# Eight value tiles projected before the key combine, which goes by column blocks, and six weight units kept in SBUF between two passes

## The chip, the cores and the metric

The kernel runs on the 8 cores of one Trainium2 chip. Each core computes 2048 of the 16384 rows of the output. Within a batch row of 4096 positions two cores share the work: both form the whole key-value sum for all 4096 rows, and each does the query side and the feed-forward part for its own half. No data pass between cores. The metric is the device time of the slowest core, in microseconds (us).

Names used below: TensorE is the matmul engine (PE in the profile), VectorE is DVE, ScalarE is ACT, GpSimd is POOL, SyncE is SP, which issues most of the DMA transfers. SBUF is the memory on the core, PSUM the matmul's result memory of 8 banks.

## The reference, cut to what matters

```python
x = x + attn(layernorm(x))          # x: (4, 4096, 1024) float32, 16 heads of 64
x = x + ffn(layernorm(x))

def attn(h):
    q = softmax((h @ Wq.T + bq) @ Wfq.T + bfq)    # over all 1024 columns
    k = softmax((h @ Wk.T + bk) @ Wfk.T + bfk)
    v = h @ Wv.T + bv
    scores = q_h @ k_h.T                           # per head, no softmax here
    return (scores / scores.sum(-1)) @ v_h

def ffn(h):                                        # weights 1024 x 4096 and back
    gate = silu(bitlinear(h, w_gate)); up = bitlinear(h, w_up)
    return bitlinear(gate * up, w_down)

def bitlinear(x, w):      # x rounded to 8 bit by row; w to {-1, 0, 1} / scale,
    ...                   # scale = 1 / mean(|w|) over the whole matrix
```

Two things follow. The two matrices of the key can be multiplied once, Wfk Wk, and so can those of the query. And since the attention has no softmax over scores, it is q (k^T v), so a 64 x 64 sum per head over all positions takes the place of the scores. The feed-forward weights need two passes: one over |w| for the mean, one that rounds with that mean.

## The kernel before, in words

The work is cut into tiles of 128 rows. A core has TKV = 32 tiles for the keys and values (16 of the other core's half, then its own 16), and TQ = 16 for the queries and the feed-forward part. All engines' programs are written out by hand as lists in order, each instruction with the events that it waits for. An engine does its list strictly in order, so an instruction that waits holds up all behind it.

First stage, weights. SyncE loads the weights in chunks of at most 128 x 1024 float32 into 8 staging buffers (`stage`), and VectorE and ScalarE cast them to bf16 in turns (`cast_chunk`, L275 and L277). Chunks 0 to 23 are Wk and Wfk, then come Wv and, from 32 on, Wq and Wfq, which overwrite the first two and so wait for the bias product BK. The key combine (L435) is 128 matmuls in two passes of 64: for each half h of the output columns all eight PSUM banks collect one row block each, while j runs over the chunks as they land. `cke` (L807, L810) copies the results out. Then come the bias item BK and the first keys.

Second stage, slots. Slot i of 32 has, on TensorE, V(i) (value projection), in slots 16 to 26 Q, in slots 4 to 12 one item of the query combine (CQ, L415 with wfT), K(i+1), the KV product of tile i (L464) and the transposes of tile i+2 (L453). Each of V, K, Q and CQ is an "item" of 16 matmuls of 128 x 512 that takes one of two PSUM areas of two banks. VectorE and ScalarE do for each tile: mean and variance (`dv_stats`), r = exp(-0.5 ln(var + eps)) (`ac_r`, L728 and L732), the normalized tile (`dv_xh`, L738), the copy of its transpose (`dv_xte`, L745), logits with bias (`dv_tk`, L750), their maximum (L754), the exponential with its sum (`ac_ek`, L1068), the reciprocal of the sum (`dv_rz`, L785) and V scaled by it (`ac_ve`, L1077 and L1084), for which the KV product waits.

The units. The feed-forward weights come in 48 units of 1 MB (16 of each matrix, w = 0 gate, 1 up, 2 down). In pass 1 ScalarE sums |w| of a unit (L335), in pass 2 GpSimd scales and rounds it (L326) and ScalarE writes it as fp8 (L348). Both passes load each unit from HBM into one of NWST = 4 buffers (`wst`). A table gives each slot its units, 74 up to slot 31: 3 a slot in slots 3 to 8, 2 in 9 to 15, 3 in 16 to 25, 2 in 26 to 31. The other 22, of the down matrix, follow in the feed-forward tiles 0 to 3.

Third stage. After slot 31 come the last queries, the first context product (L522) and 16 feed-forward tiles: gate and up (L563), silu (L1136), the product (L1013), rounding, a transpose through HBM (`s_hq`), and down (L543), three tiles late.

Of the kernel before, what the change touches and what calls it, by code (L numbers as in the profile page):

```python
# [93 lines left out]
def build_nc():  # L94
# [147 lines left out]

    chunks = []
    for j in range(CH):
        chunks += [("wk", j, 0, D, wnat), ("wfkT", j, 0, 512, wfT)]
    chunks += [("wfkT", j, 512, 512, wfT) for j in range(CH)]
    chunks += [("wvT", j, 0, D, wv) for j in range(CH)]
    for j in range(CH):
        chunks += [("wq", j, 0, D, wnat), ("wfqT", j, 0, D, wfT)]
    NK, NV = 24, 32  # L250
    chunk_id = {(c[0], c[1], c[2]): n for n, c in enumerate(chunks)}

    def cast_of(name, j, o=0):
# [1009 lines left out]
```

How the kernel before makes its waits and increments, by code:

```python
    def run(self, eng, e, sems):  # L75
        seen = {}
        for fn, after, sem, by in self.lists[eng]:
            need = {}
            for tok in after:
                assert tok.val is not None, tok.name
                if tok.val > seen.get(tok.sem, 0):
                    need[tok.sem] = max(need.get(tok.sem, 0), tok.val)
            seen.update(need)
            need = list(need.items())
            for s, v in need[:-1]:
                e.wait_ge(sems[s], v)
            inst = fn(e)
            if need:
                inst.wait_op(sems[need[-1][0]], need[-1][1], "sem-ge")
            if sem:
                inst.then_inc(sems[sem], by)
```

## Time and profile before

| | us |
|---|---|
| median of 3 runs | 1144.21 |
| lowest, highest | 1143.06, 1147.94 |
| the profiled execution | 1148.11 |
| its span, slowest core (4) | 1146.6 |
| its fastest core (1) | 1123.3 |
| TensorE busy, core 4 | 1080.8 (94%) |
| VectorE, ScalarE, GpSimd busy | 632.1, 491.1, 204.4 |

A span runs from a core's first to its last instruction. The profile is that of core 4. Matmuls are pipelined and their ends are modelled, so TensorE's busy time is not work at peak rate; the start of one group of matmuls to the start of the next is the better measure. The granted clock is given as a share of 2.4 GHz: 0.50 is the lower level, 1.2 GHz. Some matmul records are missing from a trace, which is why an item can stand there with x15.

### The profile page before, as it was taken

To read this page: it belongs to the slowest core of one execution; us is meant where nothing else is said; L and a number is where in the kernel's file an instruction comes from. 1 tells how busy PE (TensorE), PEld (TensorE's weight loads), DVE (VectorE), ACT (ScalarE), POOL (GpSimd) and SP (SyncE) were. 2 spreads that over 40 slices of the span, in tenths; PEclk is the share of its full clock that TensorE was granted. 3 is DMA by queue.
4 is the path that set the end of the run, shared out by engine and by line. 5 is a ranking of instruction groups with operands and counts; after the bars stand their busy time and mean duration, and the time that the engine had idled before them with its cause. 6 is when DMAs were issued, how large, how long until landed. Compare 5 with 4: busy or idle time off the path is not lost.

```text
span 1146.6 us, 13483 instructions; the slowest of 8 cores (1123.3 to 1146.6 us)
## 1 busy us (share of the span) xinstructions
PE 1080.8 (94%) x5379; PEld 503.7 (44%) x5414; DVE 632.1 (55%) x1140; ACT 491.1 (43%) x604; POOL 204.4 (18%) x132
## 2 busy tenths in 40 slices
PE   5859999999999999897879999999999999999998
PEld 2324454554444544342334444444444444444443
DVE  3356555667766667774826636645645645744311
ACT  2326776677787757564533123223223222222110
POOL 0000000023333330453322012012012012011010
PEclk9979899999998999998989999999999999999999
DMA  8969998689999977779971441441342351231240
GB/s 271 290 198 339 338 334 294 244 276 325 316 325 324 326 222 220 183 215 191 170 132 37 111 96 42 101 108 40 92 105 52 83 120 37 74 92 37 56 110 38
DMA packets 201263, 199.66 MB, mean 174 GB/s; under 512 B 170096, under 2 KB 170096, under 8 KB 193008
## 3 DMA queue, kind: packets, MB, share of 16 engines
q1 hardware_dynamic: 179392, 174.68, 54.2%
q10 hardware_dynamic: 21808, 24.12, 7.5%
q8 instruction: 42, 0.69, 0.3%
q14 instruction: 21, 0.17, 0.1%
HBM read 148.45 MB, written 29.36 MB: 155 GB/s over the span
## 4 chain that ended last, share of the span: by engine, by line
PE 79%; DMA 10%; DVE 4%; ACT 3%; POOL 2%; issue 1%; SPq 1%; ACTq 0%; DVEq 0%
PE ps L563 32%; PE ps L415 25%; PE ps L543 19%; DMA wst<-wdT 4%; DMA stage<-wfkT 2%; DMA wst<-wgT 2%; DMA bvb<-bv 2%; PE ps L464 1%; PE ps L453 1%; SPq L233 1%; ACT wd L348 1%; POOL hmid L1186 1%; POOL wst L326 1%; DVE hmid L1013 1%; DMA xr<-x_oth 1%
## 5 line engine op out<-in xcount | busy, mean ns | idle before, releaser
L563 PE MATMUL ps<-wg,aqT 128*128 128x512 fp8e4 x1024 | 244.9, 382 | 8.6 <-ACT silu L1136 6.0
L563 PE MATMUL ps<-wu,aqT 128*128 128x512 fp8e4 x1024 | 243.2, 381 | 4.1 <-DVE hmid L1013 4.1
L1136 ACT ACTIVATE silu<-ps,l 128x512 f32<-128x512 f32 x128 | 87.7, 686 | 319.5 <-PE ps L563 302.4
L1013 DVE SCALAR_TENSOR_TENSOR hmid<-ps,l,silu 128x512 f32<-128x512 f32 x128 | 95.7, 748 | 146.4 <-PE ps L563 102.2
L326 POOL TENSOR_SCALAR wst<-wst,msum 128x2048 f32<-128x2048 f32 x48 | 95.9, 2001 | 398.6 <-DMA wst<-wgT 292.5
L563 PEld LDWEIGHTS ps<-wu,aqT 128*128 128x128 bf16 x1024 | 100.2, 98 | 127.3 <-DVE hmid L1013 6.3
L563 PEld LDWEIGHTS ps<-wg,aqT 128*128 128x128 bf16 x1024 | 98.8, 99 | 122.4 <-ACT silu L1136 7.1
L415 PE MATMUL ps<-wck,xT 128*128 128x512 bf16 x509 | 127.8, 408 | 13.8 <-DVE xT L745 11.3
L1186 POOL TENSOR_SCALAR hmid<-hmid,hsc 128x1024 f32<-128x1024 f32 x64 | 70.4, 1118 | 306.2 <-DVE hsc L1034 306.2
L415 PE MATMUL ps<-wv,xT 128*128 128x512 bf16 x484 | 116.2, 392 | 5.7 <-ACT ek L1068 3.9
L1005 DVE SCALAR_TENSOR_TENSOR xr<-ps,hsc,xr 128x512 f32<-128x512 f32 x32 | 24.0, 751 | 168.3 <-PE ps L543 168.3
L1146 ACT ACTIVATE hqs<-hmid 128x1024 bf16<-128x1024 f32 x64 | 66.9, 1056 | 71.1 <-POOL hmid L1186 69.8
L335 ACT ACTIVATE wst<-wst 128x2048 f32<-128x2048 f32 x48 | 91.2, 1900 | 6.6 <-DMA wst<-wgT 5.2
L543 PE MATMUL ps<-wd,hqTa 128*128 128x512 fp8e4 x384 | 86.7, 387 | 6.5 <-ACT wd L348 6.5
L415 PEld LDWEIGHTS ps<-wck,xT 128*128 128x128 bf16 x512 | 52.6, 104 | 83.5 <-issue 33.8
L1021 DVE TENSOR_REDUCE hmx<-hmid 128x1 f32<-128x1024 f32 x64 | 78.1, 1220 | 2.2
L415 PEld LDWEIGHTS ps<-wv,xT 128*128 128x128 bf16 x512 | 50.1, 100 | 61.5 <-issue 13.2
L750 DVE TENSOR_TENSOR lg<-ps,bkc 128x1024 f32<-128x1024 f32 x32 | 39.2, 1224 | 60.9 <-PE ps L415 60.9
L1179 POOL TENSOR_TENSOR xr<-xr,bvb 128x1024 f32<-128x1024 f32 x16 | 38.1, 2387 | 184.7 <-DMA xr<-x_own 184.7
L543 PE MATMUL ps<-wd,hqTb 128*128 128x512 fp8e4 x320 | 69.9, 379 | 0.0
L543 PEld LDWEIGHTS ps<-wd,hqTa 128*128 128x128 bf16 x384 | 38.0, 99 | 54.2 <-ACT wd L348 7.9
L415 PE MATMUL ps<-wcq,xT 128*128 128x512 bf16 x254 | 60.6, 394 | 1.2 <-DVE hmid L750 1.1
(95 smaller groups left out, 1064.6 us busy)
## 6 DMA issues: line engine op xcount, KB each, us to landing
wst<-wgT SPq DMA_DIRECT2D x32, 1024.0 KB, 10.6
wst<-wuT SPq DMA_DIRECT2D x32, 1024.0 KB, 9.0
wst<-wdT ACTq DMA_DIRECT2D x19, 1024.0 KB, 7.0
xr<-x_own SPq DMA_DIRECT2D x32, 512.0 KB, 6.9
s_hq<-hqs SPq DMA_DIRECT2D x32, 512.0 KB, 4.1
wst<-wdT SPq DMA_DIRECT2D x13, 1024.0 KB, 8.9
xr<-x_oth SPq DMA_DIRECT2D x16, 512.0 KB, 12.1
y<-xr SPq DMA_DIRECT2D x16, 512.0 KB, 3.4
```

Source lines behind the costliest of these rows:

```text
L326: gp(lambda e: e.tensor_scalar(b, b, msum[:, 4 + w:5 + w], ROUND32, op0=ALU.mult, op1=ALU.add), [at("wld", n), at("scale", w)], ("usc", n))
L335: ac(lambda e: e.activation(b, b, ACTF.Abs, bias=0.0, scale=1.0, accum_out=absc[:, k:k + 1]), [at("wld", n)], ("unit", n))
L415: pe(lambda e, h=h, c=c, l_=l_, r_=r_: e.matmul(AB[b][:, 512 * h:512 * h + 512], l_, r_, start=(c == 0), stop=(c == CH - 1)), (list(after) ...
L543: pe(lambda e, c=c, b=b, o=o: e.matmul(KB[1 + h], b[:, o:o + 128], wd8[:, c * D + 512 * h:c * D + 512 * h + 512], start=(c == 0), stop=(c ...
L563: pe(lambda e, c=c: e.matmul(out, a[:, c * 128:c * 128 + 128], w8[:, c * DI + 512 * oc:c * DI + 512 * oc + 512], start=(c == 0), stop=(c = ...
L750: dv(lambda e: e.tensor_tensor(o, b, bias[...], op=ALU.add), after, done)
L1013: dv(lambda e: e.scalar_tensor_tensor(hmid[:, 512 * oc:512 * oc + 512], U[oc % 2], l2[:, s + 6:s + 7], sl, op0=ALU.mult, op1=ALU.mult), [a ...
L1021: dv(lambda e: e.tensor_reduce(hmx[:, s2 + k:s2 + k + 1], hmid[:, D * k:D * k + D], axis=AX, op=ALU.max, apply_absolute_value=True), [at(" ...
L1136: ac(lambda e: e.activation(silu[:, (oc % 2) * 512:(oc % 2) * 512 + 512], G[oc % 2], ACTF.Silu, bias=0.0, scale=l2[:, s + 5:s + 6]), [at(" ...
L1146: ac(lambda e: e.activation(hqs[:, g * D:(g + 1) * D], hmid[:, g * D:(g + 1) * D], ACTF.Copy, bias=-ROUND32, scale=1.0), [at("hr", t, g)] ...
L1179: gp(lambda e: e.tensor_tensor(xf(t), xf(t), bvb[...], op=ALU.add), [at("x2in", t), at("biases")], ("xb", t))
L1186: gp(lambda e: e.tensor_scalar(o, o, hsc[:, k:k + 1], ROUND32, op0=ALU.mult, op1=ALU.add), [at("hs", t)], ("hr", t, g))
```

## The change

Four things are changed.

- Loading order. x and Wv come first, interleaved, then Wfk, then Wk, then the key's bias (on a semaphore of its own), Wq and Wfq. Wk comes in column blocks: a chunk is 512 rows by 256 columns, so its rows are 1 KB long. All eight Wv casts are ScalarE's.
- V of tiles 0 to 7 (NE = 8) is projected before the combine. V0 to V3 are interleaved by landing, one bank pair for each tile. V4 to V7 follow as items, each with the transposes of the next tile ahead of it. The results are copied unscaled to SBUF as float32 (`vra`, `vrb`; L910 of the changed kernel for ScalarE), and `ac_ve` scales them from there in slots 0 to 7. `vrb` lies in the first two unit buffers.
- The key combine is eight items, one for each row block of the result, each of which needs all of Wfk and one column block of Wk.
- Units. The up matrix goes first. Units 13 to 15 of up and of gate (NRET = 3) go in pass 1 to places of their own (`keep`), in the regions where the fp8 weights will lie later, and pass 2 takes them from there without a load; the sum's unneeded output goes to `junk`. The first NB = 8 units share buffers 2 and 3. The 74 units are dealt to slots by weights of 4 for each item: 1, 1, 2, 2, 2, 3, 4, 3, 3, 3, 3, 3, 2 in slots 3 to 15, then 3, 3, 3, 4, 3, 3, 3, 3, 4, 3, 3, 2, 2, 3 in slots 16 to 29, and none in 30 and 31. The query combine is one slot later.

```diff
+NE = 8
...
+NRET = 3
...
+    vra = sb("vra", 4 * D, F32, rWC)
+    vrb = sb("vrb", 4 * D, F32, rWS)
...
+    chunks += [rows("wvT", j, wv) for j in range(CH)]
+    chunks += [rows("wfkT", j, wfT) for j in range(CH)]
+    chunks += [block(b, h) for b in range(4) for h in range(2)]
...
+        return n >= 8 and (n % 2 == 0 if n < NV else n % 4 != 3)
...
+    units = [(1, w, u) for w in (1, 0) for u in range(16)]
+    kept = list(range(16 - NRET, 16))
+    own = [(2, w, u) for w in (1, 0) for u in kept + list(range(16 - NRET))]
...
+    cq_slot = {5 + m: m for m in range(9)}
+    slot_len = [4 + (4 if i >= NE else 0) +
+                (4 if i in cq_slot or TQ <= i < TKV - DEFER else 0)
+                for i in range(TKV - 2)]
+    slot_units = {i: [] for i in range(TKV)}
+    for n in range(NA):
+        want = sum(slot_len[:3]) + (n + 1) * sum(slot_len[3:]) / NA
+        slot_units[next(i for i in range(TKV - 2) if sum(
+            slot_len[:i + 1]) >= want - 1e-6)].append(n)
...
+    NB = len([n for n in range(NA) if unit_slot[n] < NE])
+    wslot_of, k = [], 0
+    for n, (ps_, w, u) in enumerate(units):
+        if w < 2 and u in kept:
+            wslot_of.append(None)
+        elif n < NB:
+            wslot_of.append(2 + n % 2)
+        else:
+            if n == NA:
+                k = 0
+            wslot_of.append(k % (NWST if n < NA else NWF))
+            k += 1
...
+                     at("VE", 2 * s + 5) if s < 2 else None)
...
+            k = units[n][2] - 16 + NRET
+            return keep[units[n][1]][:, k * 2048:(k + 1) * 2048]
...
+        if wslot_of[n] is None:
+            if ps_ == 1:
+                sp(f"dR{w}{u}", dst, unit_src(w, u), ready[w], ("wld", n))
+            return
...
+            o = junk[...] if wslot_of[n] is None else b
...
-    for h in range(2):
-        for j in range(CH):
-            for mi in range(CH):
-                pe(lambda e, j=j, mi=mi, h=h: e.matmul(
-                    ps[:, 512 * mi:512 * mi + 512],
-                    wnat[:, j * D + mi * 128:j * D + mi * 128 + 128],
-                    wfT[:, j * D + 512 * h:j * D + 512 * h + 512],
-                    start=(j == 0), stop=(j == CH - 1)),
-                   [cast_of("wk", j), cast_of("wfkT", j, 512 * h),
-                    at("CKe", mi, 0) if h and j == 0 else None],
...
+    def pe_v4(i, j):
+        for h in range(2):
+            pe(lambda e, h=h: e.matmul(
+                ps[:, 1024 * i + 512 * h:1024 * i + 512 * h + 512],
+                xT_of(i)[:, j * 128:j * 128 + 128],
+                wv[:, j * D + 512 * h:j * D + 512 * h + 512],
+                start=(j == 0), stop=(j == CH - 1)),
+               [at("XTe", i), cast_of("wvT", j)] if h == 0 else (),
+               ("V", i) if h == 1 and j == CH - 1 else None)
+
+    x_in = [9.9, 12.9, 16.3, 21.1]
+    w_in_at = [9.8, 11.4, 14.6, 16.2, 19.4, 21.0, 22.6, 24.2]
+    order4 = [(x_in[i] - 1.4, i, -1) for i in range(4)]
+    order4 += [(max(x_in[i], w_in_at[j]), i, j) for i in range(4)
+               for j in range(CH)]
+    for _, i, j in sorted(order4):
+        if j < 0:
+            pe_xt4(i)
+        else:
+            pe_v4(i, j)
...
+    pe_xt(4)
+    for i in range(4, NE):
+        if i + 1 < NE:
+            pe_xt(i + 1)
+        pe_v(i)
+    for m in range(CH):
+        item(("CK", m), lambda c, m=m: wnat[:, c * D + m * 128:
+                                            c * D + m * 128 + 128],
+             w_rhs(wfT), [cast_of("wfkT", 7), cast_of("wfkT", 6),
+                          cast_of("wk", 2 * (m // 2)),
+                          cast_of("wk", 2 * (m // 2) + 1)],
+             ("CK", m), at("CKe", m))
+    item("BK", brep_lhs(0), w_rhs(wfT), [at("brep", 0)], ("BK",), at("BKe"))
     pe_k(0)
-    pe_xt(1)
     pe_k(1)
     for i in range(TKV):
-        pe_v(i)
+        if i >= NE:
+            pe_v(i)
...
+    sp("dC0", identb[...], id_b.ap())
+    load_x(0)
+    load_x(1)
+    load_chunk(0)
+    load_chunk(1)
+    load_x(2)
+    load_chunk(2)
+    load_chunk(3)
+    load_x(3)
+    sp("dC0", identh[...], id_h.ap(), (), ("ids",))
+    for n in range(4, 8):
         load_chunk(n)
+    for i in range(4, NE):
+        load_x(i)
     sp("dC2", b8[:, 0:CH], bk8.ap())
     sp("dC2", b8[:, CH:2 * CH], bq8.ap(), (), ("b8",))
-    for n in range(8, NK):
+    for n in range(8, NV):
...
+    def v_raw(i):
+        b = (ps[:, 1024 * i:1024 * i + 1024] if i < 4 else
+             AB[item_bank[("V", i)]])
+        evac("v" if i == 2 else "a", vraw(i), b, [at("V", i)], ("VR", i))
+
+    def cke(m):
+        evac("v" if m % 2 == 0 else "a", wck[:, m * D:(m + 1) * D],
+             AB[item_bank[("CK", m)]], [at("CK", m)], ("CKe", m))
+
+    def dv_in(i):
+        dv_stats(i)
+        ac_r(i)
...
+    casts = [[0], [1, 2], [3], [4, 5, 6, 7]]
+    for i in range(4):
+        dv_in(i)
+        for n in casts[i]:
+            cast_chunk(n)
+        dv_xte(i)
+    v_raw(0)
+    dv_in(4)
+    v_raw(1)
+    v_raw(2)
+    dv_xte(4)
+    v_raw(3)
+    for i in range(5, NE):
+        dv_in(i)
+        dv_xte(i)
+        cast_chunk(2 * i - 2)
+        cast_chunk(2 * i - 1)
+        v_raw(i - 1)
     dv_brep(0)
     dv_brep(1)
+    cast_chunk(14)
+    cast_chunk(15)
+    v_raw(NE - 1)
+    for n in range(16, 20):
         cast_chunk(n)
+    cke(0)
+    cke(1)
+    cast_chunk(20)
+    cast_chunk(21)
+    cke(2)
+    cke(3)
+    cast_chunk(22)
+    cast_chunk(23)
+    for m in range(4, CH):
+        cke(m)
...
+        b = vraw(i) if i < NE else AB[item_bank[("V", i)]]
```

How the lists change. TensorE before, from its first matmul (wfT, wnat: the key combine; wck: K; wv: V; vst, ek: KV):

```order
L435 MATMUL ps<-wfT,wnat 128x512 x128
L415 MATMUL ps<-wfT,brep 128x512 x16
L453 MATMUL ps<-identb,xh 128x128 x8
L415 MATMUL ps<-wck,xT 128x512 x16
L453 MATMUL ps<-identb,xh 128x128 x8
L415 MATMUL ps<-wck,xT 128x512 x16
L415 MATMUL ps<-wv,xT 128x512 x16
L464 MATMUL ps<-vst,ek 128x129 x8
```

TensorE now, from the end of V3 to the first K of slot 1 (xT_84 to xT_87 are tiles 4 to 7, xT_80 is tile 0):

```order
L539 MATMUL ps<-identb,xh 128x128 x16
L483 MATMUL ps<-wv,xT_84 128x512 x16
L539 MATMUL ps<-identb,xh 128x128 x8
L483 MATMUL ps<-wv,xT_85 128x512 x16
L539 MATMUL ps<-identb,xh 128x128 x8
L483 MATMUL ps<-wv,xT_86 128x512 x16
L483 MATMUL ps<-wv,xT_87 128x512 x16
L483 MATMUL ps<-wfT,wnat 128x512 x128
L483 MATMUL ps<-wfT,brep 128x512 x16
L483 MATMUL ps<-wck,xT_80 128x512 x16
L483 MATMUL ps<-wck,xT_81 128x512 x16
L550 MATMUL ps<-vst,ek 128x129 x8
```

The combine has moved behind eight value projections, and slots 0 to 7 have no V of their own any more.

ScalarE now, from the copy of V0 (vra, vrb: unscaled V; lnv and rr: Ln and Exp for the next tile's normalizing; wfT: casts of Wfk chunks). The first row of L910 is V0, the x2 are V1 and V3, then V4 and V5:

```order
L910 ACTIVATE vra<-ps 128x1024
L831 ACTIVATE lnv<-mv,cst 128x1
L835 ACTIVATE rr<-lnv 128x1
L910 ACTIVATE vra<-ps 128x1024 x2
L831 ACTIVATE lnv<-mv,cst 128x1
L835 ACTIVATE rr<-lnv 128x1
L309 ACTIVATE wfT<-stage 128x1024
L910 ACTIVATE vrb<-ps 128x1024
L831 ACTIVATE lnv<-mv,cst 128x1
L835 ACTIVATE rr<-lnv 128x1
L309 ACTIVATE wfT<-stage 128x1024
L910 ACTIVATE vrb<-ps 128x1024
```

The Ln and Exp of tile 6 stand behind the copy of V4, those of tile 7 behind the copy of V5. In before, no copy of V stood on this queue ahead of slot 0; its start was casts and copies of the combine's results.

## Rows read from the trace of the kernel before

**Rows 1.** Spans: core, first to last instruction, mean granted TensorE clock.

```profile
...
core 4: 1146.6 us, clock 0.969
...
die 0 (median of its cores): 1125.9 us, clock 0.986
die 1 (median of its cores): 1136.2 us, clock 0.974
```

**Rows 2.** Windows, core 4: busy time by engine, TensorE's clock, DMA share, GB/s.

```profile
50.00:100.00 50.00, 33.27 (x165) 15.47 (x170) 26.48 (x41) 16.47 (x28) 0.00 (x0) 0.81 0.81 253
100.00:150.00 50.00, 47.41 (x250) 22.75 (x252) 28.29 (x40) 37.33 (x51) 0.00 (x0) 0.93 1.00 335
250.00:300.00 50.00, 49.72 (x269) 24.42 (x271) 33.69 (x42) 39.75 (x44) 17.76 (x9) 0.92 0.92 297
```

**Rows 3.** Waits of TensorE, 0 to 130 us: total, times, longest.

```profile
...
PE ps L415 <- DVE xT L745: 11.3, 2, 10.2
...
```

**Rows 4.** TensorE in time, core 4: start, duration, line, operation, [idle before, releaser].

```profile
86.63 3.62 PE L415 MATMUL ps<-wck,xT 128*128 128x512 bf16 x15
90.09 0.63 PE L464 MATMUL ps<-vst,ek 128*128 128x129 bf16 x8
90.56 0.64 PE L453 MATMUL ps<-identb,xh 128*128 128x128 bf16 x8
91.02 4.37 PE L415 MATMUL ps<-wv,xT 128*128 128x512 bf16 x16
...
117.21 5.31 PE L415 MATMUL ps<-wck,xT 128*128 128x512 bf16 x16 [2.38 <-ACT vst L1084]
...
130.35 4.38 PE L415 MATMUL ps<-wck,xT 128*128 128x512 bf16 x16
...
239.37 3.62 PE L415 MATMUL ps<-wv,xT 128*128 128x512 bf16 x15
...
417.27 0.63 PE L522 MATMUL ps<-kvs,eld 128*128 128x130 bf16 x8
```

**Rows 5.** ScalarE, core 4: the last of the first 16 weight chunks.

```profile
26.67 0.63 ACT L277 ACTIVATE wfT<-stage 128x512 bf16<-128x512 f32 x1 [2.25 <-DMA stage<-wfkT]
```

**Rows 6.** VectorE in time, core 4, 27 to 135 us.

```profile
49.78 0.69 DVE L745 COPY xT<-ps 128x1024 bf16<-128x1024 bf16 x1 [2.93 <-PE ps L453]
50.39 0.80 DVE L738 TENSOR_SCALAR xh<-xr,mv,rr 128x1024 bf16<-128x1024 f32 x1
...
65.38 1.28 DVE L719 BATCH_NORM_STATS2 bnst<-xr 128x6 f32<-128x512 f32 x2
...
85.25 1.29 DVE L275 CAST wnat<-stage 128x1024 bf16<-128x1024 f32 x2
...
90.29 1.23 DVE L750 TENSOR_TENSOR lg<-ps,bkc 128x1024 f32<-128x1024 f32 x1 [2.32 <-PE ps L415]
91.55 1.22 DVE L754 TENSOR_REDUCE nm<-lg 128x1 f32<-128x1024 f32 x1
```

**Rows 7.** ScalarE in time, core 4, 27 to 135 us.

```profile
44.59 2.06 ACT L810 ACTIVATE wck<-ps 128x512 bf16<-128x512 f32 x4 [0.97 <-PE ps L435]
...
66.94 0.30 ACT L728 ACTIVATE lnv<-mv,cst 128x1 f32<-128x1 f32 x1 [18.41 <-DVE mv L722]
...
67.37 1.99 ACT L277 ACTIVATE wv<-stage 128x1024 bf16<-128x1024 f32 x2
...
92.80 1.15 ACT L1068 ACTIVATE ek<-lg,nm 128x1024 bf16<-128x1024 f32 x1 [2.39 <-DVE nm L754]
...
106.66 1.90 ACT L335 ACTIVATE wst<-wst 128x2048 f32<-128x2048 f32 x1
...
115.91 1.11 ACT L1077 ACTIVATE vst<-ps,rz 128x1024 bf16<-128x1024 f32 x1 [0.23 <-DVE rz L785]
```

**Rows 8.** Windows of 2.5 us, core 4.

```profile
92.50:95.00 2.50, 2.50 (x12) 1.02 (x10) 1.79 (x5) 1.24 (x2) 0.00 (x0) 0.81 1.01 341
117.50:120.00 2.50, 2.50 (x7) 0.87 (x6) 1.58 (x3) 2.07 (x5) 0.00 (x0) 0.50 1.01 331
```

**Rows 9.** TensorE in time, core 1.

```profile
115.19 3.63 PE L415 MATMUL ps<-wck,xT 128*128 128x512 bf16 x16 [2.54 <-ACT vst L1084]
```

**Rows 10.** DMA issues of the page: count, KB each, median us to landing.

```profile
wst<-wgT SPq DMA_DIRECT2D x32, 1024.0 KB, 10.6
...
s_hq<-hqs SPq DMA_DIRECT2D x32, 512.0 KB, 4.1
```

More of the change, by code:

```diff
@@ L191, in build_nc @@
     wst = sb("wst", NWST * 2048, F32, rWS)
+    keep = [sb("keep0", 4 * 2048, F32, rWG), sb("keep1", 4 * 2048, F32, rWU)]
+    junk = sb("junk", 2048, F8, rJK)
     xr2 = sb("xr2", 2 * D, F32, rWS + 8192 * (NWST - 1))
@@ L301, in build_nc @@
     unit_id = {k: n for n, k in enumerate(units)}
-    wslot_of = [n % NWST if n < NA else (n - NA) % NWF
-                for n in range(len(units))]
+    cq_slot = {5 + m: m for m in range(9)}
[7 more added lines that the diff above has]
+            slot_len[:i + 1]) >= want - 1e-6)].append(n)
+    unit_slot = {n: i for i, l in slot_units.items() for n in l}
+    NB = len([n for n in range(NA) if unit_slot[n] < NE])
[10 more added lines that the diff above has]
+            k += 1
     before = {}
     for n, s in enumerate(wslot_of):
+        if s is None:
+            continue
         earlier = [m for m in range(n) if wslot_of[m] == s]
-        before[n] = at("unit", earlier[-1]) if earlier else None
+        before[n] = (at("unit", earlier[-1]) if earlier else
+                     at("VE", 2 * s + 5) if s < 2 else None)
     last_x = max(m for m in range(len(units)) if wslot_of[m] == NWST - 1)
@@ L327, in unit_gp @@
                 b, b, msum[:, 4 + w:5 + w], ROUND32, op0=ALU.mult,
-                op1=ALU.add), [at("wld", n), at("scale", w)], ("usc", n))
+                op1=ALU.add),
+                [at("unit", unit_id[1, w, u]) if wslot_of[n] is None else
+                 at("wld", n), at("scale", w)], ("usc", n))
+    last_junk = [None]
     def unit_ac(n):
@@ L340, in unit_ac @@
             after = [at("usc", n)]
-            if w == 0 and u == 0:
-                after += [at("CQ", 8)]
-            if w == 1 and u == 0:
-                after += [at("cast", len(chunks) - 1),
-                          at("cast", len(chunks) - 2)]
+            if w < 2 and u == 16 - NRET:
+                after += ready[w]
             if w == 2 and u == 0:
@@ L373, in mean_dv2 @@
             op0=ALU.mult), [at("mean", w)], ("deq", w))
-    slot_units = {}
-    n0 = 0
-    for i in range(TKV):
-        left, slots = (32 - n0, TQ - i) if i < TQ else (NA - n0, TKV - i)
-        k = 0 if i < 3 else -(-left // slots)
-        slot_units[i] = list(range(n0, n0 + k))
-        n0 += k
     ffn_units = {}
@@ L389, in build_nc @@
     assert n1 == len(units)
-    unit_slot = {n: i for i, l in slot_units.items() for n in l}
     mean_at = {unit_slot[unit_id[1, w, 15]] + 1: w for w in range(2)}
@@ L399, in build_nc @@
     late_q = list(range(TQ - DEFER, TQ))
-    cq_slot = {4 + m: m for m in range(9)}
     item_no = [0]
-    bank_free = [at("CKe", 1, 1), at("CKe", 3, 1)]
-    also_free = [at("CKe", 0, 1), at("CKe", 2, 1)]
+    bank_free = [at("VR", 0), at("VR", 1)]
     item_bank = {}
@@ L417, in item @@
                     start=(c == 0), stop=(c == CH - 1)),
-                   (list(after) + [bank_free[b], also_free[b]])
+                   (list(after) + [bank_free[b]])
                    if h == 0 and c == 0 else (),
@@ L567, in pe_half @@
                after if c == 0 else (), done if c == CH - 1 else None)
-    WL = unit_id[2, 1, 15]
+    WL = max(unit_id[2, w, u] for w in range(2) for u in range(16))
     def ctx_bank(t, part):
```

179 lines of the change are left out of this document (84 added, 95 removed).

## Prediction

> **What bounds the kernel now.** I read the spans and clocks of the cores first. The time is that of the slowest core, number 4 with 1146.6 us, on the die whose clock is lower ([rows 1]). The profiled execution took 1148.11 us, 1.5 more than that span and 3.9 more than the median of the runs shown, so the sum below gives a difference, and I take it from 1144.2. Within 0.5%, 5.7 us, is what a measurement of this kernel can't tell from no change.
>
> Next I read the busy time by stage ([rows 2]). TensorE is busy for 99% of 250 to 300 us, and no wait of it stands in 130 to 400, but for 33 of 50 us in the window from 50. The first 130 us are therefore where idle time of TensorE can be won. The list of waits names the largest piece: 10.2 us of one wait for a transposed tile ([rows 3]), which stands behind the bias broadcasts that all share one semaphore. The order in time ([rows 4]) gives what I compare. The projections are items of 16 matmuls (8 for the key combine, one for its bias, 9 for the query's, 32 V, 32 K, and 13 of the 16 Q before the first context product at 417.27): 95 in all. An item takes 90.09 - 86.63 = 3.46 us, a KV product 0.47, a transpose group 0.46. When K6 starts, at 130.35, 72 of the 95 are left. In the changed order 72 are left when slot 5 begins (V0 to V7, eight combines, the bias, K0 to K5 are done). So one question decides most: is that before or after 130.35?
>
> **The change part by part: V0 to V3.** They follow the landings of x and wv. By the row where 6 MB are cast, 26.67, they would end some 2.7 us later, at 29.4 ([rows 5]). At the 335 GB/s of [rows 2] the chunks, now of 512 KB and all with whole rows, land by 22 to 23. Then TensorE itself is the limit: after x3 (4 MB in, its stats, normalizing, transpose and copy, about 21) 28 matmuls are left, 6 us. I take 27.2, and keep 25.2 and 29.4 as ends. All four V results then wait for VectorE and ScalarE.
>
> **V4 to V7.** The instruction order shows a ring here: ScalarE copies V(i-1) out of PSUM before it does the Ln and Exp for tile i+1, so XH(i+1), the transpose and then V(i) on TensorE's queue wait for V(i-1). From [rows 6] and [rows 7]: copy 1.03 (2.06 for 4 halves, two halves each), Ln and Exp 0.43 (67.37 - 66.94), XH 0.80, some 0.4 of semaphores, transposes 0.46, V itself 3.46: 6.6 us a tile, where TensorE's own work is 3.9. V4 comes first after: V0 copied 26.9, Ln and Exp for tile 4 27.4, XH 28.3, the VectorE copy of V2 29.5, transposes 30.1, XT 30.8, stats of tile 5 32.3 (1.56 from 65.38 to 66.94), Ln and Exp 32.9, XH 33.7, transposes, V4 from 34.3. Its gap is over 3 us, and such gaps have a price: after 2.38 us of wait at 117.21 the K item took 5.31 instead of 3.62, with a granted clock of 0.50, the 1.2 GHz level ([rows 4, 8]); on core 1 2.54 us of wait cost nothing ([rows 9]). So V4 ends at 34.3 + 3.4 + 1.7 = 39.4. V5 begins after 1.1 + 0.5 + 0.9 + 0.5 of copy, Ln, XH and transposes at 42.4, V6 at 48.9, V7 at 52.3, ending 55.7. The gaps before V5 and V6 are 2.6 us, between the two cases named, so I charge 1.7 us for one of them. ScalarE copies V7 and casts one more chunk: 56.8, 57.8. The key combine starts at 57.9, or at 59.6 with the charge.
>
> **The key combine.** It is 8 items, 27.6 us, then the bias item 3.5 and K0 3.4: K0 ends at 92.4. Its column blocks are loaded in rows of 1 KB, which no row of before shows. The bounds are 1.6 us for 512 KB at 335 GB/s and 4.1 us from issue to landing for the same size in rows of 256 B ([rows 10]). With either end eight of them take 13 to 33 us from 36 on, so the last pair, issued near 56, is there by 64, and is needed at 79: zero in both cases. The combine covers it; if it landed 15 us later still, it would be one for one.
>
> **Slots 0 to 4.** TensorE has only K and KV there (3.9 us), while each slot's chain is: logits 1.26, maximum 1.25, exponential 1.28, reciprocal 0.1, three casts on VectorE 1.9 ([rows 6, 7]): 5.8 us. V is already there but its scaling (1.11) still follows the exponential. K0 end +9.4 for the first KV (K1, then 5.5 us of gap, as two exponentials go ahead of it on ScalarE), K2 with a low clock +14.5, KV2 +20.3, KV3 +26.1, KV4 +31.9. So 72 are left at 124.3, with the charge at 126.0. That is 4.3 us ahead of 130.35. The 27.7 us of V work that moved into the time of loading come back almost whole as gaps: some 8 before V4, 5 before V5 and V6, 2 before the combine, 5.5 + 5 in the slots, and the lost clock.
>
> **Slots 5 to 31.** The items are the same as before, 28 to the V16 that started at 239.37, and 44 from there on. The first eight units have only two buffers. A buffer's round is landing + 1.90 for the absolute sum ([rows 7]) + 0.4 of issue. With 2.5 MB in flight at 335 GB/s each load lands 5 to 6 us after issue, the round is about 8, and the slot 7.4 to 7.9. I add 1 us. Slots 8 to 15 load 24 units and 4 MB of x in 83 us, 337 GB/s, just what [rows 2] shows as the most, but up to four units are ahead when it starts, and slot 16 loads none: zero. The six units kept save 6 MB, 18 us of transfers, from slot 16 on. On core 4 no wait of TensorE is there to be removed, so they are worth nothing to the slowest core. Slots 30 and 31 have no unit on ScalarE, where before it had two each; that frees the KV evacuation: -1 us. From 417.27 on (wd units, the hidden-tile transposes, 16 tiles) nothing differs. The junk output and the added work on POOL (none) cost nothing.
>
> **The sum.** -4.3 + 1 - 1 = -4.3 us: span 1142.3 of the profiled execution, and 1144.2 - 4.3 = 1140 as median. Its own range: the ends of V3 (-2 to +2.2), the two gaps (-1.7 to +1.7), the buffers (-1 to +2) give 1135 to 1145.
>
> **The rivals.**
> - The clock comes back in the second half (faster). Core 4 has 0.92 in three windows of 50 us from 250 on (the first stands in [rows 2]), while the other die's median is 10 us shorter ([rows 1]). If fewer transfers, or the other placing of ScalarE's units, give it full clock, 150 x 0.08 = 12 us go: 1128. Against: the items there, back to back, stay the same.
> - The buffers of the first eight units (slower). Place: slots 5 to 8, ScalarE. In before such a load took 10.6 us in the median from issue to landing ([rows 10]). With that, a round is 13 us for two units where the slot has 7.8: 5.2 x 3 = 15.6, less the 4 us that K runs ahead of KV, so 12 more: 1151. It decides from a landing of about 5.5 us. For it: the 2.38 us wait at 117.21 arose in just this way, behind a unit on ScalarE's queue. Against: 10.6 us was with four buffers in flight.
> - What is won is used up in the start (no difference). Both gaps before V5 and V6 fall to the low clock, those of 1.5 to 1.9 us in slots 2 to 4 too, and slot 14, with three units for 7.8 us of TensorE, adds 1 us: 1144 to 1145.
> - The denser stretch costs clock (slower than forecast). Core 4 was granted 0.81 at 92.5 to 95 us in dense matmuls ([rows 8]). Slots 5 to 15 should take 28 x 3.46 + 11 x 0.93 = 107.1 us and took 109.0 (130.35 to 239.37, [rows 4]), so 1.9 are lost there now. If the stretch runs at 0.92, as 250 to 300 does, 109 x 0.08 = 8.7 are lost, 6.8 more: 1147. For it: TensorE and the DMA queues are both busier there than before. Against: 150 to 250 us of before is as dense and lost little. The Trainium skill, in "TensorE: Matmul & The Clock Gate", Part 1: The HAM clock gate, has a peak-current limit of 13/16 of the clock for a die once three of its cores run dense matmuls. This trace agrees in the value, but not in the duration. Held over the 109 us, that rule would give 1140 + 20.7 - 1.9 = 1159.
>
> **How the numbers follow.** The forecast has 0.39, the returned clock 0.22, the used-up start 0.14, the buffers 0.15, the denser stretch 0.05, and 0.05 goes to something slower that is not on the list. Faster by over 0.5% means under 1138.5: 0.19 of the forecast's own share and the 0.22, so 0.41. Slower means over 1149.9: the buffers, 0.02 of the denser stretch, and the unlisted: 0.22. The rest, 0.37, is within. The range for 8 in 10 goes from the returned clock to the buffers, 1127 to 1151.
>
> **What would show it.** In the profile after: V4 starting near 34 and the combine near 58 to 60, with ScalarE's Ln between the V copies; gaps of 2.6 us before V5 and V6; a gap of some 5.5 us before the first KV; the first query combine (slot 5) at 124 to 128; V16 near 234 to 236; the first context product near 413; the same distance from there to the end, 729 us. Wrong it is if V5 and V6 follow without gaps (then the start gives 5 us more), if ScalarE waits for wst in slots 5 to 8 for more than 2 us a unit, if the clock of the second half is not 0.92, or if the wk blocks land after 79.

## The result, and the profile after

The changed kernel is slower: 1176.28 us in the median (1172.75 to 1235.38, 4 runs) against 1146.08 for the kernel before in the same runs. The ratio is 1.026, with a 95% interval of 1.0215 to 1.031. The forecast was 1140, the range ended at 1151. (The 1235.38 and a few long runs of the kernel before are disturbed ones, with a lower granted clock on one die or both; they stand in the medians, but in no ratio.)

The spans after (for [rows 1]): every core is longer than the median of either die before, and the clocks of the dies are alike.

```profile
core 4: 1171.0 us, clock 0.977
...
die 0 (median of its cores): 1159.8 us, clock 0.980
die 1 (median of its cores): 1167.8 us, clock 0.980
```

From each trace the four times below were read on all eight cores and their median formed: when slot 5's share of work is reached (72 of the 95 items left), the start of V16, the first context product, and the end. The differences from column to column tell where time is lost.

| kernel | time, median | 72 left | V16 | context | end |
|---|---|---|---|---|---|
| before | 1146.08 | 127.8 | 235.5 | 411.9 | 1130.4 |
| changed | 1176.28 | 149.4 | 262.6 | 443.0 | 1160.7 |
| difference | +30.2 | +21.6 | +27.1 | +31.1 | +30.3 |

So 21.6 us are lost before slot 5, 5.5 in slots 5 to 15, 4.0 up to the context product, and nothing behind it. The waits of TensorE over the whole span (total, times, longest) already name the places (for [rows 3]):

```profile
PE ps L550 <- ACT vst L1208: 22.0, 6, 8.6
PE ps L505 <- DMA identh<-id_h: 19.7, 1, 19.7
PE ps L483 <- ACT vst L1208: 9.5, 5, 3.7
PE ps L539 <- DVE xh L841: 8.4, 3, 3.6
```

L505 are the transposes of tiles 0 to 3: 19.7 us until an identity matrix lands. L550 are the KV products. The order in time on core 4 (for [rows 4]; the last 34 matmuls of V0 to V3, V4, transposes, V5, transposes, V6 and V7, combine, KV of tile 4, first query combine, V16, context product):

```profile
37.07 7.50 PE L513 MATMUL ps<-wv,xT 128*128 128x512 bf16 x34
...
51.87 5.72 PE L483 MATMUL ps<-wv,xT 128*128 128x512 bf16 x16
59.97 0.62 PE L539 MATMUL ps<-identb,xh 128*128 128x128 bf16 x8 [2.38 <-DVE xh L841]
60.43 3.62 PE L483 MATMUL ps<-wv,xT 128*128 128x512 bf16 x16
66.42 1.03 PE L539 MATMUL ps<-identb,xh 128*128 128x128 bf16 x8 [2.38 <-DVE xh L841]
67.25 8.32 PE L483 MATMUL ps<-wv,xT 128*128 128x512 bf16 x32
77.72 27.79 PE L483 MATMUL ps<-wfT,wnat 128*128 128x512 bf16 x128 [2.15 <-ACT wnat L309]
...
150.72 1.05 PE L550 MATMUL ps<-vst,ek 128*128 128x129 bf16 x8 [8.63 <-ACT vst L1208]
151.56 5.37 PE L483 MATMUL ps<-wfT,wnat 128*128 128x512 bf16 x16
...
265.42 3.62 PE L483 MATMUL ps<-wv,xT 128*128 128x512 bf16 x16
...
446.78 0.63 PE L620 MATMUL ps<-kvs,eld 128*128 128x130 bf16 x8
```

Part of this came out as worked out, and part did not. V4 to the combine is 77.72 - 51.87 = 25.9 us (25.3 in the prediction), with gaps of 2.38 us before the transposes for V5 and V6. Behind one of the two equal gaps the clock stayed up (16 matmuls from 60.43 in 3.62), behind the other it was low at first (32 from 67.25 in 8.32, where 7.07 is full speed). But V4 itself starts at 51.87, not 34.3. And the KV of tile 4 has an idle time of 8.63 us ahead of it, where 5.8 - 3.9 = 1.9 were expected. SyncE's queue (start, time, issues) shows both causes:

```profile
6.26 0.61 SPq L249 DMA_DIRECT2D identh<-id_h  x1
...
10.26 25.26 SPq L249 DMA_DIRECT2D xr<-x_oth  x4
...
36.51 5.99 SPq L249 DMA_DIRECT2D stage<-wfkT  x8
...
93.72 0.33 SPq L249 DMA_DIRECT2D stage<-wfqT  x1
119.48 0.33 SPq L249 DMA_DIRECT2D stage<-wq  x1
...
126.36 0.53 SPq L249 DMA_DIRECT2D wst<-wuT  x1
```

The loads of x4 to x7 take from 10.26 to 35.5, as each waits for a normalized tile, and the Wfk chunks stand behind them. The ninth Wq/Wfq chunk waits from 94 to 119 for the buffer of the first, whose cast waits for the bias item. That item is done at 109; the cast then stands on VectorE behind the logits and maxima of tiles 0 and 1 and comes at 118.77. So the first feed-forward unit (wst) is issued only at 126.36, behind eight chunks and two biases of 512 KB each that were all issued after 119. ScalarE then waits for it, with the exponential of the next tile behind:

```profile
146.02 1.91 ACT L413 ACTIVATE wst<-wst 128x2048 f32<-128x2048 f32 x1 [7.09 <-DMA wst<-wuT]
```

The identity matrices (count, KB, us to landing): the same 32 KB took 1.9 us when issued first and 13.4 when issued behind x and Wv, and the first transposes wait for both, as they share a semaphore.

```profile
identb<-id_b SPq DMA_DIRECT2D x1, 32.0 KB, 1.9
identh<-id_h SPq DMA_DIRECT2D x1, 32.0 KB, 13.4
```

The windows (for [rows 2]) show the transfer queues at 170 GB/s in 100 to 150, where before they ran at 335, and ScalarE at 41 to 42 of 50 us in 300 to 400. TensorE's clock in 250 to 300 is 1.00. That it was 0.92 on one die of the kernel before belongs to that execution: in four later kernels (units only; units and bias; units, bias, spread; bias only) the mean clock of 250 to 400 us was 0.98 to 1.00 on every core.

```profile
100.00:150.00 50.00, 33.55 (x170) 15.55 (x168) 22.94 (x30) 18.37 (x26) 0.00 (x0) 0.91 0.57 170
250.00:300.00 50.00, 50.00 (x292) 25.02 (x291) 34.11 (x51) 40.48 (x51) 7.89 (x4) 1.00 0.90 290
300.00:350.00 50.00, 46.03 (x260) 22.23 (x258) 30.81 (x42) 41.03 (x46) 19.50 (x10) 1.00 1.02 322
350.00:400.00 50.00, 48.14 (x269) 23.21 (x268) 33.27 (x42) 42.07 (x45) 20.46 (x11) 1.00 0.94 292
```

### The profile page after: what moved, and what is told of

Its sections match the earlier page's. It is cut to its first block, busy times and chain, and to the rows that moved or that the text cites. A ratio compares the mean times of both kernels' runs of the same rounds, so it can differ in the third digit from the quotient of the medians.

```text
span 1171.0 us, 13492 instructions; the slowest of 8 cores (1156.7 to 1171.0 us)
## 1 busy us (share of the span) xinstructions
PE 1076.2 (92%) x5414; PEld 503.2 (43%) x5414; DVE 624.4 (53%) x1133; ACT 499.8 (43%) x603; POOL 204.4 (17%) x132
## 4 chain that ended last, share of the span: by engine, by line
PE 61%; DMA 16%; ACT 8%; issue 7%; DVE 4%; POOL 3%; SPq 1%; ACTq 0%; DVEq 0%; POOLq 0%
PE ps L661 30%; PE ps L641 18%; PE ps L483 9%; DMA wst<-wuT 6%; DMA wst<-wdT 4%; DMA wst<-wgT 3%; POOL wst L399 2%; DMA keep<-wuT 2%; ACT wu L427 1%; DMA identh<-id_h 1%; PE ps L513 1%; ACT wst L413 1%; ACT wd L427 1%; ACT ek L1191 1%; ACT wg L427 1%
## 5 line engine op out<-in xcount | busy, mean ns | idle before, releaser
L483 PE MATMUL ps<-wck,xT 128*128 128x512 bf16 x512 | 118.4, 386 | 9.5 <-ACT vst L1208 9.5
L399 POOL TENSOR_SCALAR wst<-wst,msum 128x2048 f32<-128x2048 f32 x42 | 84.1, 2004 | 191.5 <-DMA wst<-wuT 93.2
L483 PE MATMUL ps<-wv,xT 128*128 128x512 bf16 x448 | 106.9, 394 | 0.0
L413 ACT ACTIVATE wst<-wst 128x2048 f32<-128x2048 f32 x42 | 79.9, 1902 | 20.4 <-DMA wst<-wuT 16.4
L483 PEld LDWEIGHTS ps<-wck,xT 128*128 128x128 bf16 x512 | 49.6, 99 | 73.3 <-ACT vst L1208 15.1
L483 PEld LDWEIGHTS ps<-wv,xT 128*128 128x128 bf16 x448 | 44.3, 101 | 50.8 <-issue 7.6
L483 PE MATMUL ps<-wfT,wnat 128*128 128x512 bf16 x256 | 58.5, 387 | 2.1 <-ACT wnat L309 2.1
L483 PE MATMUL ps<-wcq,xT 128*128 128x512 bf16 x256 | 57.7, 379 | 1.1 <-DVE hmid L853 1.1
```

What stands on the lines that cost most here:

```text
L399: gp(lambda e: e.tensor_scalar(b, b, msum[:, 4 + w:5 + w], ROUND32, op0=ALU.mult, op1=ALU.add), [at("unit", unit_id[1, w, u]) if wslot_of[ ...
L413: ac(lambda e: e.activation(o, b, ACTF.Abs, bias=0.0, scale=1.0, accum_out=absc[:, k:k + 1], saturate=False), [at("wld", n), last_junk[0] ...
L483: pe(lambda e, h=h, c=c, l_=l_, r_=r_: e.matmul(AB[b][:, 512 * h:512 * h + 512], l_, r_, start=(c == 0), stop=(c == CH - 1)), (list(after) ...
```

## The experiments

Each kernel was run beside the kernel before, in four groups in which that kernel's median was 1144.7 to 1146.6. The ratio is to those runs, and it can differ from the quotient of the medians by some tenths of a per cent. The four times on the right are medians of the eight cores of one profiled execution.

| kernel | time | ratio, 95% | 72 left | V16 | context | end |
|---|---|---|---|---|---|---|
| identities first | 1167.16 | 1.019 (1.011-1.027) | 140.9 | 255.0 | 436.9 | 1156.2 |
| and Ln ahead | 1167.95 | 1.020 (1.012-1.028) | 137.4 | 251.7 | 436.3 | 1159.7 |
| and units early | 1156.99 | 1.013 (1.009-1.016) | 131.2 | 244.9 | 427.4 | 1152.8 |
| and spread | 1147.19 | 1.004 (1.001-1.008) | 130.5 | 239.4 | 413.9 | 1133.0 |
| and stats ahead | 1151.10 | 1.004 (1.001-1.007) | 131.6 | 241.2 | 417.3 | 1137.3 |
| changed, spread alone | 1163.93 | 1.016 (1.012-1.021) | 150.0 | 260.0 | 432.9 | 1154.7 |
| changed, none kept | 1184.67 | 1.034 (1.030-1.038) | 148.8 | 261.8 | 452.3 | 1172.8 |
| units only | 1137.44 | 0.993 (0.990-0.995) | 125.6 | 235.9 | 407.2 | 1126.3 |
| units only, none kept | 1147.55 | 1.003 (0.999-1.006) | 126.0 | 241.9 | 418.6 | 1135.2 |
| bias only | 1130.72 | 0.988 (0.985-0.991) | 120.8 | 227.6 | 402.9 | 1117.2 |
| units and bias | 1135.72 | 0.991 (0.987-0.994) | 118.5 | 228.7 | 401.1 | 1122.5 |
| units, bias, spread | 1125.09 | 0.982 (0.978-0.986) | 116.7 | 223.6 | 393.6 | 1116.1 |

**Identities first.**

```diff
     sp("dC0", identb[...], id_b.ap())
+    sp("dC0", identh[...], id_h.ap(), (), ("ids",))
     load_x(0)
...
-    sp("dC0", identh[...], id_h.ap(), (), ("ids",))
```

> The changed kernel with one edit: both identity matrices are loaded first, ahead of x0. Theory (late identity): the first transposes stand 10 us idle until identh, which shares the semaphore, lands at 19.7 behind the chunks; XH1 to XH3 wait for it, and with them the loads of x4 to x7 and all chunks behind them on SyncE's queue. Then the start moves up by 9 to 11 us, the key combine begins near 67 instead of 77.7, and the time falls from 1176 to 1164-1168. Rival (the loads themselves are slow at the start, 6 MB by 28 us): the identity wait is covered by x1 to x3 and Wv, so the combine begins at 75 or later and the time falls by 0 to 3 us.

TensorE in time, core 4: the first transposes, those of tile 3, the last 34 of V0 to V3, the combine:

```profile
10.39 1.01 PE L505 MATMUL ps<-identb,xh 128*128 128x128 bf16 x8 [10.39 <-DVE xh L841]
...
27.29 0.61 PE L505 MATMUL ps<-identb,xh 128*128 128x128 bf16 x8
27.74 7.50 PE L513 MATMUL ps<-wv,xT 128*128 128x512 bf16 x34
...
66.48 3.79 PE L483 MATMUL ps<-wfT,wnat 128*128 128x512 bf16 x9 [2.15 <-ACT wnat L309]
```

The first transposes start at 10.39 instead of 19.7, slot 5 comes 8.5 us earlier in the medians of the cores, and the time falls by 9 us. The theory holds; the intervals of the two ratios overlap, so it is the stages that carry this. But V0 to V3 still end at 35.2, not at 27.2: tile 3's transposes are at 27.29, while x3 was reckoned ready at 21. On VectorE the statistics of a tile stand behind the copy of the transpose before it. These copies start at 11.44, 17.06, 22.29 and 27.94, so each tile costs a round of 5.2 to 5.7 us through three engines.

**And Ln and Exp ahead of the V copies.** `ac_r(i)` for tiles 6 and 7 goes ahead of `v_raw(i - 2)` on ScalarE.

> As the run before, and besides ScalarE does Ln and Exp of tiles 6 and 7 ahead of the copies of V4 and V5. Theory (ring through ScalarE, from the prediction): the gaps of TensorE before V5 and V6, 2.4 us each, and the low clock behind one of them go: 5 to 6 us less up to the key combine, 1159-1162. Rival (the Wfk and Wk chunks then bound the combine): the gaps go but reappear ahead of the combine, and the time stays within 1.5 us of the run before.

The ring is broken: the combine starts at 62.9 in the median of the cores instead of 66.7, and slot 5 comes 3.5 us earlier. The time does not follow. That is the rival's time without its cause, since no gap came back ahead of the combine (2.15 us, as before). One reason is on cores 2 and 3 of this run. A window and the combine of core 2:

```profile
60.00:95.00 35.00, 32.67 (x124) 13.46 (x125) 6.10 (x6) 7.88 (x8) 0.00 (x0) 0.81 0.62 173
```

```profile
63.71 33.77 PE L483 MATMUL ps<-wfT,wnat 128*128 128x512 bf16 x125 [2.15 <-ACT wnat L309]
```

The combine's 128 matmuls took 33.8 us on cores 2 and 3, at a granted clock of 0.81. They took 27.8 on core 6, and 29.5 on the other five, which had a low clock only behind the gap of 2.15 us. On cores 2 and 3 the 0.81 did not end with the combine: in windows of 10 us it is the level up to 210 us, less only where TensorE had waited, and V16 came at 263.9 and 263.3 there, against 249 to 254 on the other six. In one more of the four executions these two cores had the lowest mean clock (0.959 and 0.966, the others 0.976 to 0.982). That the denser stretch costs clock was a rival of the prediction. Here it held on two cores, so I can't say what it costs on the average.

The peak-current limit of the Trainium skill ("TensorE: Matmul & The Clock Gate", Part 1) agrees with this row in value, 13/16, but not in place: it is said to take a whole die, and cores 0 and 1 of this die had 1.00 from 70 to 90 us, in the middle of the same combine. The traces of the changed kernel and of the runs before and behind this one had 0.96 to 1.00 in 160 to 250 us (cores 0, 2, 4 and 6).

**And the first two units early.**

```diff
+    unit_load(0)
+    unit_load(1)
     for n in range(NV, NV + 8):
         load_chunk(n)
```

> The second run's kernel (identities first, Ln ahead of the V copies) and besides the loads of the first two units stand ahead of the first Wq chunk on SyncE's queue. Theory (the first units are late since SyncE stands behind chunks that wait for the bias item): the 7 to 9 us in which TensorE waits ahead of the KV product of tile 4 go, that product starts 28.6 - 8 = 21 us after the first one instead of 28.6, and slot 5 begins near 130; 1160-1163. Rival (the ring of two buffers then binds): the wait moves to slots 5 to 7 and V16 begins as before, near 252; 1166-1169.

TensorE, core 4 (KV of tile 0, KV of tile 4, first query combine):

```profile
108.17 1.05 PE L550 MATMUL ps<-vst,ek 128*128 128x129 bf16 x8 [5.42 <-ACT vst L1216]
...
130.71 0.64 PE L550 MATMUL ps<-vst,ek 128*128 128x129 bf16 x8 [1.61 <-ACT vst L1216]
131.19 3.61 PE L483 MATMUL ps<-wfT,wnat 128*128 128x512 bf16 x16
```

The idle time of 8.6 us is 1.61 now. From the start of the first KV product to slot 5 are 23.0 us, as in the prediction (31.9 less 9.0; its 9.4 is the product's end). Here the sum's terms hold, once the two omitted waits are gone. By the medians 11 us of time went. In the medians of the cores it is 6 us at slot 5 and 7 to 9 behind it; part of the rest may be the low clock of two cores in the run compared with.

**And the units spread over slots 3 to 31.** `range(TKV - 2)` becomes `range(TKV)` in the dealing.

> As the run before it in this list, with the 74 units dealt over slots 3 to 31 instead of 3 to 29, by the same weights. Theory (ScalarE is overfilled in slots 16 to 29): V16 to the first context product takes 174 to 177 us instead of 181 to 184, and the time falls by 4 to 7 us against the run with the early units. Rival (waiting for ScalarE there is set by the slots' own chain): the stretch stays over 180 and the time within 2 us.

10 us. V16 comes 5.5 us earlier and V16 to the context product takes 174.5 instead of 182.5. The same edit alone on the changed kernel:

> The changed kernel with one edit: the 74 units are dealt over slots 3 to 31 instead of 3 to 29. Theory (the dealing alone overfills ScalarE, whatever the start): as in the pair measured before, 9 to 11 us less, 1165-1168. Rival (it paid only since the first units came early): under 4 us, 1172-1176.

12 us. Core 4 from 265 to 430 us, changed and spread:

```profile
265.00:430.00 165.00, 157.00 (x893) 76.39 (x890) 103.45 (x138) 135.81 (x152) 59.69 (x30) 1.00 0.96 302
```

```profile
265.00:430.00 165.00, 162.07 (x924) 79.64 (x923) 106.30 (x144) 136.03 (x154) 55.99 (x29) 1.00 0.93 302
```

ScalarE is as busy, but TensorE does 924 instead of 893 matmuls in the same stretch. The overfilled ScalarE holds the exponentials and V scalings, and TensorE waits for them. In 160 to 430 us it waited so for 9.5 + 1.1 us in the changed kernel (the 9.5 is the L483 row above), and for 2.3 + 0.7 with the units spread:

```profile
PE ps L483 <- ACT vst L1208: 2.3, 3, 1.3
```

**And the statistics ahead.** In the loop over tiles 0 to 3, `dv_stats(i + 1)` and `ac_r(i + 1)` go ahead of `dv_xte(i)`. With that, Ln and Exp of tile i + 1 also go ahead of the Wv casts that stood between the two.

> The kernel with all three mends (identities first, Ln ahead of the V copies, first units early) and the spread dealing, and besides the statistics, Ln and Exp of tiles 1 to 3 come ahead of the copy of the transpose before them. Theory (what is left of the late start is the chain of 5.6 us a tile through VectorE, TensorE and ScalarE): V3 ends 4 to 6 us earlier, near 30, the combine begins at 57-59 instead of 62.4, and the time is 1141-1144. Rival (the landings of the chunks bound V0 to V3): the combine begins within 1.5 us of 62.4 and the time stays at 1146-1148.

It missed; the rival's outcome, though not its cause. TensorE, core 4 (the second pair of matmuls of V0, tile 3's transposes, the last 34 matmuls), and the second Wv cast on ScalarE with the Ln ahead of it:

```profile
16.91 1.03 PE L513 MATMUL ps<-wv,xT 128*128 128x512 bf16 x2 [3.29 <-ACT wv L309]
...
27.79 0.61 PE L505 MATMUL ps<-identb,xh 128*128 128x128 bf16 x8
28.23 7.50 PE L513 MATMUL ps<-wv,xT 128*128 128x512 bf16 x34
```

```profile
15.37 0.29 ACT L834 ACTIVATE lnv<-mv,cst 128x1 f32<-128x1 f32 x1 [2.85 <-DVE mv L828]
...
15.81 1.99 ACT L309 ACTIVATE wv<-stage 128x1024 bf16<-128x1024 f32 x2
```

The last 34 matmuls start at 28.23, where they started at 28.41 in the same kernel without the edit. The edit took one wait away and made another. The statistics of tile 2 wait for x2 until 13.81, its Ln stands behind them, and the second Wv cast behind the Ln: 15.81, where it was at 14.70. TensorE waits for it until 16.91, and from 19.6 on it has no idle time up to the end of V3. So the theory is not tested cleanly. The chain through VectorE was not alone; the Wv casts on ScalarE and TensorE's fixed order, which expects tile 3 at 21.1, hold V0 to V3 as well. No run separates the three.

**The changed kernel with nothing kept.** `NRET = 0`; the wait ahead of the first rounded unit of a matrix goes with it, to unit 0.

> The changed kernel with NRET = 0: no unit is kept, pass 2 loads all again; the dealing of units to slots 3 to 29 stays. Theory (ScalarE, not the transfers, holds slots 17 to 29): 6 MB more to load change the time by under 4 us. Rival (transfers hold them): 6 MB more at 335 GB/s are 18 us in slots that are already full, and the time rises by 8 to 18 us over 1176.

8.4 us more (1184.67), with V16 unmoved and all of it between V16 and the context product (190.5 instead of 180.4 us). The rival holds: the kept units do pay, and without them the transfers hold that stretch.

**Units only.** The kernel before with the part on units: order, `keep`, dealing; its start untouched. V in every slot gives slots a weight of 8 or 12, so 35 units go into slots 3 to 15 and 39 into 16 to 29.

> The kernel before with the second half of the change alone: up matrix first, three units each of up and gate kept in SBUF, units dealt over slots 3 to 29 by weight. Its start is that of the kernel before (the query combine at slot 4, V in every slot). Theory (ScalarE is overfilled): with 42 pass-2 and down units in 14 slots instead of 16, the exponentials and V scalings come late and TensorE waits for them some 10 us in slots 17 to 29; the time is 3 to 8 us over the kernel before, 1149-1154. Rival (the saved 6 MB relieve the queues): TensorE's waits from slot 16 on fall below those before (2 to 6 us) and the time is 3 to 6 us under it, 1140-1143.

The rival again, and beyond its range: 0.7% faster than the kernel before. Core 4, 300 to 350 us:

```profile
300.00:350.00 50.00, 46.68 (x259) 22.73 (x262) 33.15 (x40) 40.17 (x45) 19.65 (x10) 1.00 0.86 275
```

The queues have slack there, 0.86 where the kernel before had 0.99. With nothing kept:

> The third run's kernel with NRET = 0: the up matrix first and the new dealing stay, nothing is kept. Theory (the 6 MB that are not loaded again are the gain): the time is at or above the kernel before, 1145-1152. Rival (the new order and dealing are the gain, the last two slots free): 1137-1141 as with the kept units.

No difference from the kernel before (0.999 to 1.006). So the 6 MB are the gain of this part, 10 us, and the order and dealing by themselves give none.

**Units and bias.** As units only, and the biases each on a semaphore of its own, as in the changed kernel.

> The third run's kernel (start of the kernel before, kept units) and besides the key's bias has a semaphore of its own, so that the bias sum does not wait for the two biases loaded 14 us later. Theory (that wait is the largest piece of the start, 10 us, and the low clock behind it adds 2): K1 starts near 55 instead of 65, and the time falls by 6 to 11 us below the third run, to 1127-1131. Rival (the tile 2 loads and the Wv casts, which stand behind it anyway, take its place): 0 to 3 us, 1134-1137.

K1, TensorE, core 4, in the kernel before (its wait is that of [rows 3]) and now:

```profile
64.92 5.91 PE L415 MATMUL ps<-wck,xT 128*128 128x512 bf16 x16 [10.24 <-DVE xT L745]
```

```profile
58.76 3.63 PE L451 MATMUL ps<-wck,xT 128*128 128x512 bf16 x16 [2.80 <-DVE xT L781]
```

The wait shrinks to 2.8 us and slot 5's work is reached 7 us earlier. The time fell by 1.7 us only, less than the theory's 6 to 11 and within the intervals of the pair, so this pair leaves open how much arrives at the end. The bias part alone, on the kernel before:

> The kernel before with one part of the change alone: each bias has a semaphore of its own. Theory (the 10 us wait of K1 is on the path of all that follows): K1 starts near 58 instead of 64, V16 7 us earlier, and the time falls by 6 to 9 us, to 1137-1140. Rival (the transfers of the units, saturated from 250 to 400 us in the kernel before, give the gain back): the first context product moves by under 3 us, and the time by 0 to 3.

14 us in the medians, ratio 0.985 to 0.991: more than the 7 us by which K1 moved. The end of core medians is 13.2 us earlier, the context product 9.0. Of the rest, 3.9 us lie in feed-forward tiles 0 to 3, where the edit changes nothing. From the context product to the end the kernels of the table differ by up to 11 us (714.3 to 725.4), though no edit aims at it, so a difference of this size may be scatter; its cause stays open.

**Units, bias, spread.** The best version.

> The kernel with the old start, kept units and the key's bias on its own semaphore, with the units dealt over slots 3 to 31. Theory (the last slots have room on ScalarE): 2 to 5 us below the same kernel with slots 3 to 29, 1131-1134, ratio 0.986-0.989. Rival (with V in every slot the dealing to 29 was already loose, and late units now delay the down matrix): no difference, 0.990-0.993.

1125.09 us, 1.8% under the kernel before (0.978 to 0.986), and 51 us under the changed one. That is 6 us below the theory's range. It has the change's units and bias semaphores, and leaves out the rest: the loading order, V before the combine, the combine by column blocks and the two buffers of the first units.

## Why the prediction was wrong

The point of comparison was right: the 72 items decided. The sum to it was not. On core 4 slot 5 began at 151.56 instead of 126.0. Of these 25.6 us, 17.4 were there when V3 ended, 7.4 came in slots 0 to 4, and 0.8 between them.

- **V0 to V3, "I take 27.2, and keep 25.2 and 29.4 as ends".** They ended at 44.6 on core 4. This step failed, for two reasons. It left out what the transposes wait for besides the tile: the identity load, moved behind x3 on the queue and sharing its semaphore (shown: 9.3 us on this core, 8.5 in the medians at slot 5, 9 us of time). And "x3 about 21" was the time of one tile's chain, not of four rounds of 5.2 to 5.7 us. I had listed TensorE's and ScalarE's order and not VectorE's. With the Wv casts and TensorE's fixed order it makes the other 8.0 us (35.2 against 27.2); this is argued from the trace, and the one run that went for the chain did not gain them.
- **V4 to V7, the combine, K0.** Right to within 1 us each, the charge for one low clock of two gaps included. The combine did not wait for Wk in blocks of 1 KB rows (128 matmuls in 27.79 us).
- **Slots 0 to 4, 31.9 us.** The chain was right (23.0 of 22.9 with early units, and a first gap of 5.42 us where 5.5 were worked out). Its units were costed as if their loads were there. I had followed the queue past the waits only from slot 5 on. Units 0 and 1 stand behind chunks that wait for the bias item and for VectorE's order: 8.6 us idle (shown; 6 to 9 us in the medians of the cores).
- **Slots 5 to 15, "I add 1 us".** 5.5 us in the medians. The load of the queues was mis-sized. 2.5 MB at 335 GB/s are 7.5 us and not "5 to 6" (eleven unit loads of 148 to 190 us landed in 7.6 in the median). And 24 units of 1024 KB with 4 MB of x in 83 us are 354 GB/s and not 337, more than the most that [rows 2] shows. The largest piece is a wait for ScalarE that every core has (1.4 to 3.7 us at its longest), on core 4 with a low clock behind it. Slot 9 has four units, ScalarE waits there for the loads of two kept ones, and the next tile's exponential and V scaling stand behind them. ScalarE and TensorE, core 4:

```profile
202.31 1.91 ACT L413 ACTIVATE junk<-keep 128x2048 fp8e4<-128x2048 f32 x1 [2.68 <-DMA keep<-wuT]
```

```profile
209.82 5.24 PE L483 MATMUL ps<-wck,xT 128*128 128x512 bf16 x16 [3.67 <-ACT vst L1208]
```

Spreading leaves three units in slot 9 and two fewer in slots 3 to 15. It gives 4.8 us of this stretch back with the first units early and 3.2 alone.

- **Slots 16 to 31, "they are worth nothing" and "-1 us".** Both wrong. The freed last two slots were paid for by 14 fuller ones: 10 to 12 us of time, 7.5 to 8 of them in this stretch (shown twice). The kept units are worth 8 to 10 us (shown twice). I judged them by core 4 of one execution, where with a clock of 0.92 TensorE had no wait for ScalarE. On core 0 of the other die, at 0.99, it waited 5.9 us for the scaled V in 160 to 430:

```profile
PE ps L415 <- ACT vst L1084: 5.9, 2, 5.1
```

- **From the context product on, no difference.** 1160.7 - 443.0 is 717.7, and 718.5 before: right.

The rival of the two buffers had the right sign and the right engine (ScalarE behind a unit), but the wrong cause, and the wait was at the KV product of tile 4 and not in slots 5 to 8, where core 4 had no wait of TensorE for ScalarE. The rival of the returned clock had its condition and not its effect. Core 4 was granted 1.00 where it had 0.92, and took 181.4 us from V16 to the context product where it had taken 177.9. Cores 0 to 3 of the kernel before took 172.6 to 175.2 at 0.99 to 1.00, so the full clock was worth 3 to 5 us there and not 12: with it TensorE waits for ScalarE instead.

The four mends take 29 of the 30 us back by the medians, and some 25 by the ratios (1.026 to 1.004). Then the changed kernel's start is still 22 us behind the same units, bias and dealing with the old start: 13.8 us at slot 5 and 20.3 at the context product. What follows is an explanation from the traces and not shown by a run of its own; the loading order, the column blocks and the two buffers differ between the two kernels as well. In the old start V(i) fills TensorE while tile i's exponential is under way: from the first to the fifth KV product it does 9 items in 34.8 us. With V gone from these slots it does 4 items in 22.6. And the eight V items during loading take from 12.6 to some 60 us, as each tile has to pass three engines first, while the combine needs only a cast per chunk and ran in 7.2 to 45.5, during loading too.

## What to carry to other kernels

Work that is brought forward to fill the loading time must itself be free of chains, and it must not be the filler of a chain later: count what the engine will do in the place it was taken from. When loads are reordered, follow every queue past each wait to the first transfer of every consumer, small constants and shared semaphores included. And a slot left free at the end is paid for by the others: deal work by the engine that is fullest, not by the one that is being waited for.

## What the runs showed of the hardware

- The landing of a small transfer depended on what was issued ahead of it: 32 KB landed in 1.9 us as the first and in 13.4 behind eight transfers of 512 KB. A unit of 1 MB, issued at 126.36 behind 5 MB issued since 119.48, was there at 146.
- The granted clock after equal gaps was once full and once half: after 2.38 us in the changed kernel (60.43 and 67.25 above), and after 2.15 us ahead of the combine with Ln ahead (128 matmuls in 27.8 us on core 6, in 29.5 on five cores; in the changed kernel in 27.8 on seven cores of eight). After 5.42 and 8.63 us it was 0.50 at first (the 8 matmuls of a KV product in 1.05 us instead of 0.63), the 1.2 GHz level.
- Two cores of a die were held at 0.81 in one execution, from the combine to 210 us, while their two neighbours and the other die had 1.00 in the middle of the combine.
